# Where an expert's token list is made in a mixture-of-experts layer, and how many semaphores its gathers count on

## The chip, the cores and the metric

The kernel runs on one NeuronCore of one Trainium2 chip. The metric is device time in microseconds (us) for one launch, the median of several runs. One further launch was recorded by the hardware profiler; all rows shown here come from that one.

The engines are called as the profile calls them: PE is the matrix engine (PEld its weight loads), DVE the vector engine, ACT the scalar engine, POOL the GpSimd engine, SP the sync engine, which here only issues DMAs. DMAs that POOL issues run in one queue, those of SP in another.

## The reference

```python
x = x + tanh(g_xattn[0]) * xattn(layernorm(x), ctx_512, ...)      # (32, 112, 256), 16 heads, 375 keys
x = x + tanh(g_ffn[0])   * ffn(layernorm(x), Wg, W1, b1, W2, b2)

def ffn(x, Wg, W1, b1, W2, b2):          # 3584 tokens, 8 experts, k = 896 tokens of each
    S = sigmoid(xt @ Wg).T
    G, I = top_k(S, k)
    ex = xt[I]
    hid = gelu(einsum('ekh,ehf->ekf', ex, W1) + b1[:, None, :])          # 256 -> 1024
    out = (einsum('ekf,efh->ekh', hid, W2) + b2[:, None, :]) * G[..., None]   # 1024 -> 256
    return zeros_like(xt).at[I.reshape(-1)].add(out.reshape(-1, h))
```

Every expert takes its own 896 best tokens, so a token may be taken by several experts or by none.

## The kernel before

The program has four stages one after the other: constants and queries, attention, routing (scores, then a search for each expert's threshold, to about 694 us of the span), and `experts`, to the end. The change is in `experts` alone.

**Tiles of an expert.** Its 896 tokens are 7 groups of 128 rows (`NG`), in two chunks: groups 0 to 3 and groups 4 to 6 (`CHUNK`). Each float32 operand is held as a high and a low part, and each product is three matmuls. The first product (L1266) has 16 rounds of six matmuls: `k = 8 * c + f`, 8 blocks of 128 hidden columns for each chunk. ACT takes each round through Gelu twice (L1156, L1157), DVE subtracts to get the low part (L1203, tile `hl`). The second product (L1278) has 24 matmuls for each of the 7 groups; DVE adds the bias (L1219), ACT multiplies by the gate (L1162), and POOL adds the 128 rows into the output in HBM with an indirect DMA, the scatter (L1133).

**What an expert needs.** Its token list: `list_start` (six DVE instructions, L751 to L761) writes one-hot tiles, `list_rows` (L768, four times) writes masks, `list_products` (L779) is 32 small PE matmuls in four groups of eight, and `list_end` (five DVE instructions, L791 to L796) makes the row numbers `T.idx` and the gates `T.gate`. POOL then copies both (L1120, L1121), and issues seven indirect DMAs, the gathers (L1125), one for each group of 128 rows, from HBM to `ex`. PE transposes `ex` (L1295), ACT and DVE split it into `exh` and `exl` (L1168, L1225). Weights: SP loads W1 and W2 (1 MB each, L815 and L817) into one pair of buffers as soon as the last low part of the weights that lay there is made; ACT makes the high part (L804) and DVE the low part (`weights_low`, L811) in the second product of the expert before.

**The order.** Each engine runs a function `step` for s = -1 to 7, where `live(0)` is expert s, `live(1)` work for expert s + 1, `live(2)` for expert s + 2. Steps 1 to 4 are a hardware loop, the others are written out. Before the change, expert s + 2's list is made in step s: `list_start` after round 1 of the first product, masks after rounds 4, 7, 10 and 13, the 32 matmuls between groups 1 and 2 of the second product, `list_end` after `result(2)`. Expert 0's list is made in routing, expert 1's in step -1, in one piece, while expert 0's rows are gathered. The gathers of expert s + 1 are issued at the start of step s on POOL, ahead of the scatters of expert s.

On PE the second product of a step is: groups 0 and 1, list matmuls, groups 2 and 3, a wait for all seven gathers (`gathered`), transposes of chunk 0, group 4, transposes of chunk 1, groups 5 and 6. On DVE it is `result(g)` and `weights_low` part g for g = 0 to 3, then `tokens_low(0)`, `result(4)`, `tokens_low(1)`, `result(5)`, `result(6)`. All queues are in order.

Of the kernel before, what the change touches and what calls it, by code (L numbers as in the profile page):

```python
# [18 lines left out]
NG = CAP // 128  # L19
# [744 lines left out]
def list_rows(dve, T, at, j):  # L764

    n = B // 4
    wait(dve, T.l_used, at(4, j - 3))
    dve.tensor_tensor(T.L[j][:], T.iota_l[:].unsqueeze(1).to_broadcast([LQ, n, 128]),  # L768
                      T.place_e[:, 1, j * n:(j + 1) * n].unsqueeze(2).to_broadcast([LQ, n, 128]), ALU.is_equal)\
       .then_inc(T.l_ready, 1)  # L770


def list_products(pe, T, at, pR, j):
    pe.wait_ge(T.l_ready, at(4, j + 1))
    if j == 0:
        pe.wait_ge(T.listing, at(LISTING, 6))
    for b in range(B // 4):
        k = j * (B // 4) + b
        last = pe.matmul(pR[:, 0:5 * NG], T.L[j][:, b, :], T.A[:, k].rearrange("p c g -> p (c g)"),  # L779
                         start=(k == 0), stop=(k == B - 1))  # L780
    last.then_inc(T.l_used, 1)
# [258 lines left out]
def experts(nc, T, xn, W1, b1, W2, b2, out):  # L1040

    CHUNK = [(0, 4), (4, NG)]
    with ExitStack() as ctx:
        sem = Sems(nc, ctx, "e")

# [15 lines left out]
        p1, p2, pT, pR = banks("p1", 3), banks("p2"), banks("pT"), banks("pR", 1)[0]  # L1061
        b1_loaded, b1_t, b1_c, b1_e = sem("b1_loaded"), sem("b1_t"), sem("b1_c"), sem("b1_e")
        b2_loaded = [sem("b2_loaded0"), sem("b2_loaded1")]
        gathered, added = sem("gathered"), sem("added")
        xt_ready, xh_done, xl_done = sem("xt_ready"), sem("xh_done"), sem("xl_done")
        h_ready, hh_done, hl_done = sem("h_ready"), sem("hh_done"), sem("hl_done")
        y_ready, y_read, y_done, passed = sem("y_ready"), sem("y_read"), sem("y_done"), sem("passed")
# [15 lines left out]
        def count(i, r, off, per, add):  # L1083
            return i * (2 * per) + ((r + off) * per + add)

        def of(i, r, off):

            return lambda per, add: count(i, r, off, per, add)
# [22 lines left out]
        @block.gpsimd  # L1111
        def _(pool):
            def step(i, r, live):
                if live(1):
                    p = (r + 1) % 2

                    wait_alone(pool, y_done, count(i, r, -1, NG, NG), passed)
                    wait_alone(pool, added, count(i, r, -1, 16 * NG, 16 * NG), passed)
                    wait_alone(pool, T.listing, count(i, r, 1, LISTING, LISTING), passed)
                    pool.tensor_copy(idx[p][:], T.idx[:]).then_inc(T.idx_ready, 1)  # L1120
                    pool.tensor_copy(gate[p][:], T.gate[:]).then_inc(T.idx_ready, 1)  # L1121
                    wait_alone(pool, T.idx_ready, count(i, r, 1, 2, 2), passed)
                    wait_alone(pool, xt_ready, count(i, r, 0, 4, 4), passed)
                    for g in range(NG):
                        pool.indirect_dma_start(out=ex[:, g, :], out_offset=None, in_=xn,  # L1125
                                                in_offset=bass.IndirectOffsetOnAxis(ap=idx[p][:, g:g + 1], axis=0))\
                            .then_inc(gathered, 16)
                if live(0):

                    wait_alone(pool, added, count(i, r, -1, 16 * NG, 16 * NG), passed)  # L1130
                    for g in range(NG):
                        wait_alone(pool, y_done, count(i, r, 0, NG, g + 1), passed)
                        pool.indirect_dma_start(out=out, out_offset=bass.IndirectOffsetOnAxis(ap=idx[r % 2][:, g:g + 1], axis=0),  # L1133
                                                in_=y[g][:], in_offset=None, compute_op=ALU.add).then_inc(added, 16)

            run(pool, step)
            pool.wait_ge(added, NE * NG * 16)
# [51 lines left out]
        @block.vector  # L1189
        def _(dve):  # L1190
            def step(i, r, live):
                new = of(i, r, 2)

                def at(per):
                    return count(i, r, 2, per, 0)

                if live(0):
                    for c, (g0, g1) in enumerate(CHUNK):
                        n = (g1 - g0) * 128
                        for f in range(8):  # L1200
                            k, cols = 8 * c + f, slice(g0 * 128, g1 * 128)
                            dve.wait_ge(hh_done, count(i, r, 0, 16, k + 1))
                            dve.tensor_tensor(hl[:, f, cols], hid[k % 4][:, 0:n], hh[:, f, cols].bitcast(F32),  # L1203
                                              ALU.subtract).then_inc(hl_done, 1)
                            if live(2) and k == 1:
                                list_start(dve, T, new, at)
                            if live(2) and k in (4, 7, 10, 13):
                                list_rows(dve, T, new, (k - 4) // 3)
                    dve.wait_ge(b2_loaded[r % 2], fills(i, r, 0, 16, 16))
                elif live(2):  # L1210
                    list_start(dve, T, new, at)
                    for g in range(4):
                        list_rows(dve, T, new, g)
                    list_end(dve, T, new, pR)

                def result(g):
                    dve.wait_ge(y_ready, count(i, r, 0, NG, g + 1))
                    wait(dve, added, count(i, r, -1, 16 * NG, 16 * NG))
                    dve.tensor_tensor(y[g][:], p2[g % 2][:, 0:D], b2s[r % 2][:], ALU.add).then_inc(y_read, 1)  # L1219

                def tokens_low(c):
                    g0, g1 = CHUNK[c]
                    for kk in range(2):
                        dve.wait_ge(xh_done, count(i, r, 1, 4, 2 * c + kk + 1))
                        dve.tensor_tensor(exl[:, kk, g0 * 128:g1 * 128], pT[kk][:, 0:(g1 - g0) * 128],  # L1225
                                          exh[:, kk, g0 * 128:g1 * 128].bitcast(F32), ALU.subtract).then_inc(xl_done, 1)

                if live(0):
                    for g in range(4):
                        result(g)  # L1230
                        if live(1):
                            weights_low(dve, T, (r + 1) % 2, of(i, r, 1), g)
                        if live(2) and g == 2:
                            list_end(dve, T, new, pR)
                if live(1):
                    tokens_low(0)
                if live(0):
                    result(4)
                if live(1):
                    tokens_low(1)  # L1240
                if live(0):
                    result(5)
                    result(6)

            run(dve, step)

        @block.tensor
        def _(pe):
# [4 lines left out]
            def step(i, r, live):  # L1253
                if live(0):
                    wh, wl = T.w1h[r % 2], T.w1l[r % 2]
                    pe.wait_ge(T.w_low, count(i, r, 0, 4, 4))
                    for c, (g0, g1) in enumerate(CHUNK):
                        n, cols = (g1 - g0) * 128, slice(g0 * 128, g1 * 128)
                        pe.wait_ge(xl_done, count(i, r, 0, 4, 2 * c + 2))
                        for f in range(8):  # L1260
                            if 8 * c + f >= 3:
                                pe.wait_ge(hh_done, count(i, r, 0, 16, 8 * c + f - 2))
                            fs, j = slice(f * 128, (f + 1) * 128), 0
                            for k in range(2):
                                for w, v in ((wh, exh), (wh, exl), (wl, exh)):
                                    last = pe.matmul(p1[(8 * c + f) % 3][:, 0:n], w[:, k, fs], v[:, k, cols], start=(j == 0), stop=(j == 5))  # L1266
                                    j += 1
                            last.then_inc(h_ready, 1)

                def second(g0, g1):  # L1270
                    for g in range(g0, g1):
# [7 lines left out]
                                j += 1  # L1279
                        last.then_inc(y_ready, 1)  # L1280

                new = of(i, r, 2)
                if live(0):
                    second(0, 2)
                if live(2):
                    for j in range(4):
                        list_products(pe, T, new, pR, j)
                if live(0):
                    second(2, 4)

                def transposes(c):
                    for kk in range(2):
# [4 lines left out]
                        last.then_inc(xt_ready, 1)  # L1297

                if live(1):
                    pe.wait_ge(gathered, count(i, r, 1, 16 * NG, 16 * NG))  # L1300
                    transposes(0)
                if live(0):
                    second(4, 5)
                if live(1):
                    transposes(1)
                if live(0):
                    second(5, NG)
# [46 lines left out]
```

## Time and profile before

| | us |
|---|---|
| median of 3 runs (1063.42 to 1067.46) | 1063.61 |
| the profiled execution | 1062.17 |
| its span, first to last instruction | 1060.4 |
| PE busy over the span | 885.8 (84%) |
| DVE / ACT / POOL busy | 698.5 / 616.3 / 227.5 |
| granted PE clock, mean of the span | 0.928 of full |

Times in the rows are us from the start of the span. In a timeline the first number is the start and the second the length. For a row with "x2" or more it is the length of them together. A bracket at the end gives the idle time before the instruction and what ended it. The granted clock is 1.00 at 2.4 GHz and 0.50 at 1.2 GHz.

### The profile page before, as it was taken

Reading aid. Unit: us, or ns where it says so; the run is one execution under the profiler, and the core shown is the slowest. Engines: PE = TensorE matmul, PEld = TensorE weight load, DVE = VectorE, ACT = ScalarE, POOL = GpSimd, SP = SyncE. Lnnn points to the kernel's source line nnn. Section 1 sums busy time; section 2 is a strip of 40 time slices with the busy share of each in tenths; the row PEclk is TensorE's granted clock in tenths of the full one; section 3 lists DMA queues with packets and bytes.
Section 4 is the critical chain, followed back from the end, with each engine's and each line's share of the span. In section 5 each row is a group of like instructions: output and inputs, shape, how many; then the busy total and the mean of one; then the engine's idle time right before and its main releaser. Section 6 shows DMA issues by size and latency. Waiting matters only on the chain. (4 is left out here: it accounts for less than half of the span.)

```text
span 1060.4 us, 23352 instructions
## 1 busy us (share of the span) xinstructions
PE 885.8 (84%) x8843; PEld 700.0 (66%) x8843; DVE 698.5 (66%) x1884; ACT 616.3 (58%) x1305; POOL 227.5 (21%) x192
## 2 busy tenths in 40 slices
PE   0763789999999999999999850039999999999995
PEld 0331357767676776777676640029999999999995
DVE  6681267787778777877878648857566576574540
ACT  1432477777777777777776531009568476485671
POOL 1343000000000000000000004042556466565313
PEclk9986699999999999999999975559999999999998
DMA  2211674565566456546644012031533524525203
GB/s 69 70 35 35 154 161 116 143 156 124 118 156 143 122 131 157 129 121 147 151 114 101 24 34 77 0 127 34 125 83 95 128 46 123 128 49 137 40 11 35
DMA packets 96209, 104.63 MB, mean 99 GB/s; under 512 B 11744, under 2 KB 92272, under 8 KB 96112
## 3 DMA queue, kind: packets, MB, share of 16 engines
q1 hardware_dynamic: 84128, 88.50, 33.5%
q0 software_dynamic: 10752, 14.69, 8.1%
q8 instruction: 65, 1.06, 0.4%
q10 hardware_dynamic: 1232, 0.12, 0.1%
q14 instruction: 32, 0.26, 0.1%
HBM read 39.60 MB, written 14.68 MB: 51 GB/s over the span
## 5 line engine op out<-in xcount | busy, mean ns | idle before, releaser
L405 DVE TENSOR_REDUCE a_nm<-a_pS 112x1 f32<-112x375 f32 x512 | 264.7, 543 | 122.8 <-PE a_pS L500 119.8
L350 ACT ACTIVATE a_P<-a_pT 128x448 f32<-128x448 f32 x384 | 209.2, 546 | 136.0 <-PE a_pT L494 135.3
L500 PE MATMUL a_pS<-kst,a_qst 96*112 96x375 bf16 x512 | 151.9, 336 | 3.6 <-DVE a_nm L405 3.1
L494 PE MATMUL a_pT<-a_qst,kst 98*128 98x112 bf16 x1536 | 139.3, 213 | 1.6 <-DMA a_qst<-a_mT 1.5
L494 PEld LDWEIGHTS a_pT<-a_qst,kst 98*128 98x128 bf16 x1536 | 107.4, 99 | 42.7 <-issue 8.6
L1278 PE MATMUL e_p<-w2h,e_hh 128*128 128x256 f32 x448 | 128.3, 286 | 0.0
L1278 PE MATMUL e_p<-w2h,e_hl 128*128 128x256 f32 x448 | 126.2, 282 | 0.0
L1278 PE MATMUL e_p<-w2l,e_hh 128*128 128x256 f32 x448 | 126.2, 282 | 0.0
L358 ACT ACTIVATE kp<-a_pK,bk 128x375 bf16<-128x375 f32 x192 | 109.5, 570 | 19.1 <-PE a_pK L524 12.1
L1133 POOL DMA_INDIRECT out_dram<-e_y,e_idx x56 | 88.3, 1577 | 134.0 <-ACT e_y L1162 130.3
L879 POOL MEMSET r_factors<- 128x1 f32 x15 | 0.6, 98 | 540.2 <-POOLq L236 539.9
L1203 DVE TENSOR_TENSOR e_hl<-e_hid,e_hh 128x384 fp32r<-128x384 f32 (+1 forms) x128 | 77.7, 623 | 52.9 <-ACT e_hh L1157 52.2
L511 PE MATMUL a_pO<-a_P,V 128*32 128x112 f32 (+1 forms) x3072 | 100.9, 264 | 0.3 <-ACT a_P L350 0.3
L1266 PE MATMUL e_p<-e_exh,w1h 128*128 128x512 f32 (+1 forms) x256 | 94.8, 370 | 0.0
L1266 PE MATMUL e_p<-e_exl,w1h 128*128 128x512 f32 (+1 forms) x256 | 94.5, 369 | 0.0
L1266 PE MATMUL e_p<-e_exh,w1l 128*128 128x512 f32 (+1 forms) x256 | 94.5, 369 | 0.0
L1125 POOL DMA_INDIRECT e_ex<-xn_scratch,e_idx x56 | 82.8, 1478 | 27.3 <-issue 15.6
L1156 ACT ACTIVATE e_hid<-e_p,e_b1e 128x384 f32<-128x384 f32 (+1 forms) x128 | 81.5, 637 | 9.7 <-PE e_p L1266 1.5
L1278 PEld LDWEIGHTS e_p<-w2l,e_hh 128*128 128x128 f32 x448 | 84.7, 189 | 0.0
L1278 PEld LDWEIGHTS e_p<-w2h,e_hl 128*128 128x128 f32 x448 | 84.5, 189 | 0.0
L1278 PEld LDWEIGHTS e_p<-w2h,e_hh 128*128 128x128 f32 x448 | 84.1, 188 | 0.0
L511 PEld LDWEIGHTS a_pO<-a_P,V 128*32 128x32 f32 (+1 forms) x3072 | 69.8, 110 | 21.6 <-issue 20.3
(193 smaller groups left out, 1506.3 us busy)
## 6 DMA issues: line engine op xcount, KB each, us to landing
kst<-kp SPq DMA_DIRECT2D x192, 192.0 KB, 3.6
w<-in_L_ffn_W_dram SPq DMA_DIRECT2D x16, 1024.0 KB, 7.5
a_qst<-qp SPq DMA_DIRECT2D x96, 112.0 KB, 3.8
a_craw<-in_ctx_dram SPq DMA_DIRECT2D x32, 128.0 KB
q_xin<-in_x_dram SPq DMA_DIRECT2D x8, 448.0 KB, 3.8
a_xb<-in_x_dram SPq DMA_DIRECT2D x32, 112.0 KB, 3.2
out_dram<-a_x SPq DMA_DIRECT2D x32, 112.0 KB, 2.5
xn_scratch<-a_x SPq DMA_DIRECT2D x32, 112.0 KB, 2.6
```

What stands on the lines that cost most here:

```text
L350: act.activation(P[quad % 2][:, c, :], pT[u % 2][:, 0:4 * LQ], ACT.Exp).then_inc(exp_done, 1)
L358: act.activation(kp[b % 2][:, part, t, 0:LK], pK[:, 0:LK], ACT.Identity, bias=T.bk[:, t:t + 1])\
L405: dve.tensor_reduce(nm[:, h:h + 1], pS[h % 2][0:LQ, 0:LK], AXX, ALU.max, negate=True).then_inc(s_used, 1)
L494: last = pe.matmul(pT[u % 2][:, j * LQ:(j + 1) * LQ], kst[b % 4][:, h, c * 128:(c + 1) * 128], q_of(b, slice(None), h), start=True, stop=True)
L500: pe.matmul(pS[h % 2][0:LQ, 0:LK], q_of(b, slice(0, ROWS), h), kst[b % 4][0:ROWS, h, 0:LK], start=True, stop=True).then_inc(s_ready, 1)
L511: last = pe.matmul(pO[VW * j:VW * (j + 1), quad * LQ:(quad + 1) * LQ], V[b % 2][0:n, c, 4 * quad + j, :], P[quad % 2][0:n, c, j * LQ:(j + ...
L1125: pool.indirect_dma_start(out=ex[:, g, :], out_offset=None, in_=xn, in_offset=bass.IndirectOffsetOnAxis(ap=idx[p][:, g:g + 1], axis=0))\
L1133: pool.indirect_dma_start(out=out, out_offset=bass.IndirectOffsetOnAxis(ap=idx[r % 2][:, g:g + 1], axis=0), in_=y[g][:], in_offset=None, c ...
L1156: act.activation(hid[k % 4][:, 0:n], p1[k % 3][:, 0:n], ACT.Gelu, bias=b1e[:, f:f + 1])
L1203: dve.tensor_tensor(hl[:, f, cols], hid[k % 4][:, 0:n], hh[:, f, cols].bitcast(F32), ALU.subtract).then_inc(hl_done, 1)
L1266: last = pe.matmul(p1[(8 * c + f) % 3][:, 0:n], w[:, k, fs], v[:, k, cols], start=(j == 0), stop=(j == 5))
L1278: last = pe.matmul(p2[g % 2][:, 0:D], v[:, f, rows], w[:, f, :], start=(j == 0), stop=(j == 23))
```

## The change

The list of expert s + 1 is made in step s instead of step s - 1, all of it before the second product. `list_start` comes after round 0, the masks after rounds 3, 6, 9 and 11, and PE's four groups of eight list matmuls after rounds 6, 9, 12 and 14 of the first product. `list_end` comes on DVE after the last `hl` of the first product, ahead of `result(0)`. Step -1 makes no list. The gathers count on two semaphores: groups 0 to 3 on `gathered[0]`, groups 4 to 6 on `gathered[1]`; PE waits for the second only ahead of the transposes of chunk 1. POOL's order is the same: copies, seven gathers, seven scatters.

```diff
+    ROWS_AT, LISTED_AT = [3, 6, 9, 11], [6, 9, 12, 14]
-        gathered, added = sem("gathered"), sem("added")
+        gathered, added = [sem("gathered0"), sem("gathered1")], sem("added")
@@ gpsimd
-                            .then_inc(gathered, 16)
+                            .then_inc(gathered[int(g >= CHUNK[1][0])], 16)
@@ vector
-                new = of(i, r, 2)
+                new = of(i, r, 1)
                 def at(per):
-                    return count(i, r, 2, per, 0)
+                    return count(i, r, 1, per, 0)
...
-                            if live(2) and k == 1:
+                            if live(1) and k == 0:
                                 list_start(dve, T, new, at)
-                            if live(2) and k in (4, 7, 10, 13):
-                                list_rows(dve, T, new, (k - 4) // 3)
+                            if live(1) and k in ROWS_AT:
+                                list_rows(dve, T, new, ROWS_AT.index(k))
+                    if live(1):
+                        list_end(dve, T, new, pR)
                     dve.wait_ge(b2_loaded[r % 2], fills(i, r, 0, 16, 16))
-                elif live(2):
-                    list_start(dve, T, new, at)
-                    for g in range(4):
-                        list_rows(dve, T, new, g)
-                    list_end(dve, T, new, pR)
...
-                        if live(2) and g == 2:
-                            list_end(dve, T, new, pR)
@@ tensor
                             last.then_inc(h_ready, 1)
+                            if live(1) and 8 * c + f in LISTED_AT:
+                                list_products(pe, T, of(i, r, 1), pR, LISTED_AT.index(8 * c + f))
...
-                new = of(i, r, 2)
                 if live(0):
-                    second(0, 2)
-                if live(2):
-                    for j in range(4):
-                        list_products(pe, T, new, pR, j)
-                if live(0):
-                    second(2, 4)
+                    second(0, 4)
...
                 if live(1):
-                    pe.wait_ge(gathered, count(i, r, 1, 16 * NG, 16 * NG))
+                    pe.wait_ge(gathered[0], count(i, r, 1, 16 * 4, 16 * 4))
                     transposes(0)
                 if live(0):
                     second(4, 5)
                 if live(1):
+                    pe.wait_ge(gathered[1], count(i, r, 1, 16 * 3, 16 * 3))
                     transposes(1)
```

## Rows read from the trace of the kernel before

**Rows 1.** The chain that ended last, in order: start, us, what.

```profile
705.33 3.59 DMA e_ex<-xn_scratch,e_idx
...
711.55 1.69 PE e_pT L1295 x6
713.24 21.34 PE e_p L1266 x96
...
757.15 19.58 PE e_p L1266 x96
776.73 5.75 PE e_p L1278 x48
782.48 0.82 PE e_pR L779 x32
783.30 5.84 PE e_p L1278 x48
789.14 0.87 PE e_pT L1295 x8
790.01 2.87 PE e_p L1278 x24
...
987.49 11.52 PE e_p L1278 x96
```

**Rows 2.** Timeline of POOL, the copies and gathers ahead of expert 0.

```profile
694.94 0.24 POOL L1120 COPY e_idx<-idx 128x7 int32<-128x7 int32 x1 [41.64 <-POOLq L826]
...
695.81 1.33 POOL L1125 DMA_INDIRECT e_ex<-xn_scratch,e_idx  x1 [0.50 <-POOL e_gate L1121]
...
701.57 0.95 POOL L1125 DMA_INDIRECT e_ex<-xn_scratch,e_idx  x1 [0.30 <-issue]
```

**Rows 3.** Timeline of DVE, expert 1's masks in step -1.

```profile
696.96 4.62 DVE L768 TENSOR_TENSOR L<-iota_l,place_e 112x1024 bf16<-112x1024 f32 x4
```

**Rows 4.** Timeline of DVE in step 1, whose first product ends at 776.73.

```profile
777.38 1.03 DVE L1203 TENSOR_TENSOR e_hl<-e_hid,e_hh 128x384 fp32r<-128x384 f32 x2
...
780.08 1.22 DVE L811 TENSOR_TENSOR w1l<-w,w1h 128x1024 fp32r<-128x1024 f32 x1
...
787.77 0.19 DVE L791 COPY rt<-e_pR 128x35 f32<-128x35 f32 x1
...
788.70 0.40 DVE L796 TENSOR_SCALAR gate<-gate,gf 128x7 f32<-128x7 f32 x1
```

**Rows 5.** Timeline of POOL in step 3, a copy and a gather beside DVE work.

```profile
848.19 1.45 POOL L1121 COPY e_gate<-gate 128x7 f32<-128x7 f32 x1
850.66 2.50 POOL L1125 DMA_INDIRECT e_ex<-xn_scratch,e_idx  x1 [1.03 <-issue]
```

**Rows 6.** Timeline of DVE in the same stretch of step 3.

```profile
848.30 1.29 DVE L1203 TENSOR_TENSOR e_hl<-e_hid,e_hh 128x512 fp32r<-128x512 f32 x2
...
851.57 0.69 DVE L1203 TENSOR_TENSOR e_hl<-e_hid,e_hh 128x512 fp32r<-128x512 f32 x1
```

**Rows 7.** Timeline of SP's queue, weight loads issued in steps -1 and 0.

```profile
696.21 0.38 SPq L815 DMA_DIRECT2D w<-in_L_ffn_W_dram  x1
...
748.86 0.39 SPq L815 DMA_DIRECT2D w<-in_L_ffn_W_dram  x1
```

**Rows 8.** DMA issue to landing, us, issued at 695.8, 714.0, 745.4 and 749.2.

```profile
e_ex<-xn_scratch,e_idx POOLq DMA_INDIRECT x1, 7.7
...
e_ex<-xn_scratch,e_idx POOLq DMA_INDIRECT x1, 2.7
...
out_dram<-e_y,e_idx POOLq DMA_INDIRECT x1, 3.8
...
out_dram<-e_y,e_idx POOLq DMA_INDIRECT x1, 8.3
```

**Rows 9.** Stretches: length, busy of PE, PEld, DVE, ACT, POOL, clock, DMA share, GB/s.

```profile
1048.00:1051.00 3.00, 0.88 (x8) 0.68 (x6) 0.42 (x1) 0.51 (x1) 1.68 (x2) 1.00 0.37 44
1051.00:1052.00 1.00, 0.00 (x0) 0.00 (x0) 0.00 (x0) 0.00 (x0) 0.71 (x1) 0.77 0.00 0
```

## The prediction

> **What bounds the kernel now.** I read the chain of waits first, since it says which stage the change can move. From 713.24 to the last matmul it is PE alone [rows 1]: in the whole stage PE never waits, and a step lasts 42.15 us, 19.58 of it the first product. So whatever the change puts on PE, or makes PE wait for, is paid in full, and what it speeds on other engines in the steps gives nothing. The reader is to see one more thing in the chain: ahead of the first expert it runs over the gathers and their last landing, at 708.92 (705.33 + 3.59), then 4.3 us of transposes and splits before the first product [rows 1]. There the change can win. The timelines of POOL and DVE then show what lies beside these pieces, and the DMA issues with their landings what a gather costs at different times.
>
> I write E for the end of a step's first product (776.73 in step 1, [rows 1]) and give later times as E + x.
>
> **Ahead of the first expert: a gain of 4.0.** The seven gathers are issued from 695.81; the first took 1.33 us, the fourth 0.95 and each has 0.30 idle before it [rows 2]. The slow ones lie beside expert 1's masks on DVE [rows 3], which go. At 1.25 each the fourth starts at 699.56 instead of 701.57 and the seventh at 703.32 instead of 705.33. The weights are in flight then (issued at 696.21, [rows 7]), so landings don't move as far as issues; I take the seventh at 707 (bounds: 2.7 after its issue, 706.0, by the gather without a load beside it [rows 8], and 708.9, unmoved). With the second semaphore the transposes of chunk 0 and their splits run before that: they took from 708.96 to 711.51 for the half that the next transposes wait for. Only the last 1.69 us of transposes stays behind the landing [rows 1]. With the fourth landed at 705 the first product starts at about 707.5 + 1.7 = 709.2, not 713.24: 4.0 won. Ends: 2.6 (708.9 + 1.7) and 5.5.
>
> **PE's list work: 2.4 lost.** Groups 0 to 3 of the second product take 5.75 + 0.82 + 5.84 with the list between them and 11.52 without [rows 1]: 0.89 for a list, of which 0.07 is the seam. Six lists lay in steps before, seven do now: 0.9. Four seams in place of one: 3 x 0.07 x 7 = 1.5. Whether the masks are ready costs nothing if they are: the fourth, after round 11, would be done about 18.6 us into the step and PE asks for it after round 14, at about 19.3; the others have 0.5 to 1.0 us too. If that cover is gone, each late mask costs its lateness, up to 0.5 in four places of seven steps; I take the sum as 0.9 to 6.
>
> **The new wait: 34 lost.** This is the heart. List and gathers of expert s + 1 were a step ahead; now they start when the first product has ended, and PE asks for the first four gathers 11.5 us later, at E + 11.5, and for the last three 0.87 + 2.87 us after that, at E + 15.3 [rows 1]. Followed step by step:
> - The last `hl` ends at E + 1.7. `list_end` takes 1.33 (787.77 to 789.10), so the list is ready at E + 3.0 in the loop; a written-out step has 0.23 in place of 0.40 for its last instruction and is ready at E + 2.75 [rows 4].
> - POOL's copy starts 0.3 later. A POOL copy beside DVE's subtraction is held until that ends: it took 1.45 and ended at 849.64, the subtractions at 849.59 [rows 5, 6]. In the new place DVE starts the first `weights_low` at E + 3.35 and ends it at E + 4.57 [rows 4]. In the loop the gate's copy meets it; 1.0 us of waits follows [rows 5]: first gather at E + 5.7. In a written-out step the copy is through, and the first gather itself is held to E + 4.5.
> - A gather that starts beside a subtraction is held the same way: 2.50 instead of 0.95, up to the end of the one that ends at 852.26 [rows 5, 6]. The next `weights_low` parts lie at about E + 6.1, 9.1 and 11.95, 1.22 each. With 1.25 a gather and these holds, the fourth works from E + 8.5 (loop: 10.1), the seventh from E + 13.05 (loop: 14.3).
> - The fourth lands 2.7 to 2.8 later [rows 8]: at E + 11.3, in time; in the loop at E + 13.0, 1.5 late.
> - The seventh meets the weights. SP issues their load when the fourth `weights_low` ends: at 748.86 in step 0, E + 14.3 [rows 7], and now 0.8 to 0.9 sooner, at E + 13.4, since no list stands in the second product. A gather issued 0.4 before such a load landed after 7.7 instead of 2.7. A scatter issued 0.4 behind it landed after 8.3 instead of 3.8 [rows 7, 8]. I take 7.0 to 7.3 after issue: E + 20.2, and E + 21.3 in the loop. PE asks at E + 15.3 and at E + 16.8 there: it waits 4.8 and 4.5.
>
> The sum: steps 0 and 5, 4.8 each; steps 1 to 4, 6.0 each; step 6 has no load left, 0.6: 34.2. Bounds: with every landing at 2.7 and no copy held it is 0 to 0.6 a step, under 4 in all; with 8.3 it is 45.
>
> By the row the POOL queue stands nearly still while the weights pour in. The Trainium skill, "DMA: Bandwidth & Descriptors", section "Queues, rings and completion order", says otherwise: each DMA engine goes round its queues and changes after a packet, so a gather would wait for a packet or so of the weights and land within a microsecond of its usual time. That would make the sum the one of the first rival.
>
> **PE's clock: 11 lost.** The granted clock was 1.00 (2.4 GHz) until PE had done its last matmul at 1048.9, and fell in the slice from 1051, mean 0.77, with PE idle from the one to the other [rows 9]. A wait of 4.5 to 5 us in six steps is longer than that idle time and should bring it to 0.50 each time. The nearest price is the first product of expert 0, begun at the low level: 21.34 instead of 19.58 [rows 1], so 1.8 a time, 10.8 for six. Ends: nothing, and 20 if the low stretch covers twice that work.
>
> What else moves costs nothing that I can see. POOL's seven scatters stand behind the gathers and end at about E + 29 instead of E + 26; they are asked for when the next step's list is copied, at E + 45. The second product's DVE work loses `list_end` from its middle. The first product's DVE work is the same, shifted by a round.
>
> **Sum.** 1062.2 (profiled) - 4.0 + 2.4 + 34.2 + 10.8 = 1105.6. The median of the runs is 1.4 above the profiled one: 1107.0.
>
> **Rivals.**
> - *The gathers slip past the weights* (the other side). They land 2.7 to 3.6 after issue, because the seventh is ahead of the load by a few tenths, or since it gets its turn. For it: the scatter at 745.4, 3.5 us ahead of a load, had its usual 3.8 [rows 8]. Against it: the seventh starts only 0.35 ahead, nearer to the gather that took 7.7. Then the waits are 0.3 to 0.6 a step, the clock stays: 1063.6 - 4.0 + 2.4 + 4 = 1066. The point from which it decides is the seventh gather working by about E + 12, in place of 13.05. 0.15.
> - *The same, and everything in time:* no wait, PE's seams free: 1063.6 - 5.5 + 0.9 = 1059, and 1058 with the clock up sooner in the first product. 0.05.
> - *Only the loop's late start costs.* No meeting with the weights, but the held copy and 1.8 a step in four steps: 9 + 2.4 - 4.0: 1071. 0.12.
> - *Forecast:* the weights catch the seventh gather in at least steps 0 to 5. Without the clock's loss 1096, with stalls of 6 and the larger clock price 1124. 0.68.
>
> **Chances and range.** A measurement of this kernel can tell about 0.5%, 5.3 us. Faster by more than that: 0.05, the second rival. Within it: 0.15, the first. Slower: 0.80, the other two. The range from 1066 to 1122 takes in the third and half of the first, and leaves out its upper end, where every unknown is dear; the forecast's own range is 1086 to 1122.
>
> **What would show it.** In the changed kernel's chain: the first product of expert 0 starts near 709; gathers stand in the chain of every step; PE's transposes of chunk 1 wait 4 to 5 us in steps 0 to 5 and under 1 in step 6; the landing of the gathers issued last in a step is near 7 in the first six. Stretches of 0.50 clock follow these waits. The forecast is wrong if DVE doesn't hold POOL (all gathers issued by E + 12.5), or if those landings stay near 3.

## The result, and the profile after

| | before | after |
|---|---|---|
| median of 6 runs each | 1063.69 us | 1096.03 us |
| ratio | 1 | 1.0297, 95% interval 1.0271 to 1.0323 |
| profiled execution / its span | 1062.17 / 1060.4 | 1094.03 / 1092.3 |
| PE busy (share of the span) | 885.8 (84%) | 897.3 (82%) |

The change costs 32.3 us, 3.0%. The forecast was 1107, 11 us too much; its range held. The ratios here and below leave out a run that lies over 1.5% above the fastest of its kernel; that happened once, in `a_w2_first`.

PE was busy for 11.5 us more, and the rest of the time is in waits. Those of PE from 700 us on are these (who waited, for whom: us in total, times, longest):

```profile
PE e_pT L1287 <- DMA e_ex<-xn_scratch,e_idx: 29.3, 9, 8.9
PE e_pT L1287 <- DVE e_exl L1223: 0.7, 1, 0.7
```

8.9 of the 29.3 lie ahead of expert 0, where the kernel before had 6.9. The other 20.4 are new. The chain shows where (start, us, what), from the end of step 1's first product, which I call E as in the prediction (780.08):

```profile
780.08 8.65 PE e_p L1276 x72
...
791.44 0.95 POOL e_ex L1126
792.39 0.30 issue
792.69 6.10 DMA e_ex<-xn_scratch,e_idx
798.79 0.05 issue
798.84 1.02 PE e_pT L1287 x6
799.86 7.10 PE e_p L1276 x48
806.96 9.82 PE e_p L1262 x42
816.78 0.21 PE e_pR L779 x8
817.00 3.58 PE e_p L1262 x18
820.58 0.21 PE e_pR L779 x8
820.79 3.23 PE e_p L1262 x18
824.02 0.21 PE e_pR L779 x8
824.23 2.17 PE e_p L1262 x12
826.40 0.21 PE e_pR L779 x8
826.62 1.16 PE e_p L1262 x6
```

The reader is to see three things against [rows 1]. A gather, the seventh, now stands in the middle of the second product, with 6.10 us from issue to landing. Behind it 48 matmuls take 7.10 us, not 5.75. And the list's four groups of eight stand in the first product, which lasts 20.82 (806.96 to 827.77) instead of 19.58.

POOL's timeline of that step, with SP's queue behind it:

```profile
783.00 0.19 POOL L1121 COPY e_idx<-idx 128x7 int32<-128x7 int32 x1 [20.91 <-DVE gate L796]
783.13 0.18 POOL L1122 COPY e_gate<-gate 128x7 f32<-128x7 f32 x1
784.31 1.24 POOL L1126 DMA_INDIRECT e_ex<-xn_scratch,e_idx  x1 [1.00 <-POOL e_gate L1122]
...
788.56 0.96 POOL L1126 DMA_INDIRECT e_ex<-xn_scratch,e_idx  x1 [0.30 <-issue]
...
792.69 1.31 POOL L1126 DMA_INDIRECT e_ex<-xn_scratch,e_idx  x1 [0.30 <-issue]
```
```profile
793.42 0.37 SPq L815 DMA_DIRECT2D w<-in_L_ffn_W_dram  x1
793.99 0.37 SPq L817 DMA_DIRECT2D w<-in_L_ffn_W_dram  x1
```

The DMA issues with their landings, for the gathers issued at 791.44, 792.69 and 1031.17 (the seventh of step 6, which loads no weights):

```profile
e_ex<-xn_scratch,e_idx POOLq DMA_INDIRECT x1, 2.7
...
e_ex<-xn_scratch,e_idx POOLq DMA_INDIRECT x1, 6.1
...
e_ex<-xn_scratch,e_idx POOLq DMA_INDIRECT x1, 3.2
```

Neighbours 1.25 us apart in one queue land after 2.7 and after 6.1. The weight load is issued 0.73 behind the second of them. In steps 0 to 5 the seventh gather landed after 5.5, 6.1, 5.9, 6.0, 6.5 and 6.0 us.

The clock, in three stretches behind that wait (length, busy of PE, PEld, DVE, ACT, POOL, clock, DMA share, GB/s):

```profile
794.00:799.00 5.00, 1.62 (x14) 1.41 (x13) 0.81 (x2) 0.51 (x1) 4.08 (x4) 1.00 0.87 293
799.40:802.80 3.40, 3.40 (x18) 3.40 (x17) 1.03 (x2) 0.96 (x2) 2.79 (x3) 0.50 1.17 278
802.80:806.90 4.10, 4.10 (x36) 4.10 (x35) 0.42 (x1) 0.51 (x1) 1.63 (x2) 1.00 0.63 83
```

After a stretch with 1.62 us of work in 5, PE had 1.2 GHz for about 3.4 us, with 18 matmuls in 3.4 us, and then 36 in 4.1. In the second product one matmul started 0.21 us after another at the low level, and 0.12 at the high one. There is one such stretch after the wait in each of steps 1 to 5, and none in step 0, whose wait came as 1.2 and 1.45 us in two pieces. The first piece was for the fourth gather, which landed 4.2 us after its issue, with no weight load issued by then; the trace names no reason.

**Where the 29.6 us went.** From the first gather's issue to the last matmul the kernel before took 353.1 us (695.81 to 1048.90), the one after 382.7 (698.04 to 1080.78). The 2.2 by which that first issue came later lie in routing, which the change doesn't touch.

| part | predicted | measured |
|---|---|---|
| ahead of expert 0 | -4.0 | -2.6 |
| list matmuls: 7 x 1.24 less 6 x 0.89 | +2.4 | +3.3 |
| first product of expert 0, clock up sooner (20.7 from its first matmul without the list, not 21.7) | 0 | -1.0 |
| PE's waits for gathers, steps 0 to 6: 2.7, 3.4, 3.3, 3.4, 3.9, 3.4, 0.5 | +34.2 | +20.4 |
| low clock: 5 stretches, about 1.5 each | +10.8 | +7.4 |
| not placed (0.3 a step) | | +2.1 |

### The profile page after: what moved, and what is told of

Its sections match the earlier page's. It is cut to its first block and busy times, and to the rows that moved or that the text cites. A ratio compares the mean times of both kernels' runs of the same rounds, so it can differ in the third digit from the quotient of the medians.

```text
span 1092.3 us, 23365 instructions
## 1 busy us (share of the span) xinstructions
PE 897.3 (82%) x8843; PEld 705.2 (65%) x8843; DVE 698.5 (64%) x1884; ACT 616.9 (56%) x1305; POOL 201.7 (18%) x192
## 5 line engine op out<-in xcount | busy, mean ns | idle before, releaser
L1276 PE MATMUL e_p<-w2h,e_hh 128*128 128x256 f32 x448 | 131.2, 293 | 0.0
L1276 PE MATMUL e_p<-w2h,e_hl 128*128 128x256 f32 x448 | 129.9, 290 | 0.0
L1276 PE MATMUL e_p<-w2l,e_hh 128*128 128x256 f32 x448 | 129.4, 289 | 0.0
L358 ACT ACTIVATE kp<-a_pK,bk 128x375 bf16<-128x375 f32 x192 | 109.5, 570 | 19.1 <-PE a_pK L524 12.1
L1157 ACT ACTIVATE e_hid<-e_p,e_b1e 128x384 f32<-128x384 f32 (+1 forms) x128 | 81.6, 637 | 17.8 <-PE e_p L1262 10.8
L1276 PEld LDWEIGHTS e_p<-w2l,e_hh 128*128 128x128 f32 x448 | 88.6, 198 | 0.0
L1276 PEld LDWEIGHTS e_p<-w2h,e_hh 128*128 128x128 f32 x448 | 88.0, 197 | 0.0
L1276 PEld LDWEIGHTS e_p<-w2h,e_hl 128*128 128x128 f32 x448 | 87.8, 196 | 0.0
L1163 ACT ACTIVATE e_y<-e_y,e_gate 128x256 f32<-128x256 f32 x56 | 28.5, 508 | 99.1 <-DVE e_y L1217 99.1
```

The lines of the kernel that those rows point to most:

```text
L358: act.activation(kp[b % 2][:, part, t, 0:LK], pK[:, 0:LK], ACT.Identity, bias=T.bk[:, t:t + 1])\
L1157: act.activation(hid[k % 4][:, 0:n], p1[k % 3][:, 0:n], ACT.Gelu, bias=b1e[:, f:f + 1])
L1276: last = pe.matmul(p2[g % 2][:, 0:D], v[:, f, rows], w[:, f, :], start=(j == 0), stop=(j == 23))
```

## The experiments

Ratios are to the kernel before, run on the same chip. The runs of one kernel scatter over some 8 us, so the steps are compared by their traces.

**1. The load behind the gathers** (`a_load_late`): one more wait of SP in the kernel after.

```diff
                     wait_alone(sp, T.w_low, count(i, r, 0, 4, 4), passed)
+                    wait_alone(sp, gathered[1], count(i, r, 0, 16 * 3, 16 * 3), passed)
                     load_weights(...)
```

> The changed kernel, but SP also waits for the last three gathers of expert s before it issues the load of expert s + 1's weights. Theory (the weight load holds up the seventh gather in POOL's queue): the seventh gather lands 2.7 to 3.2 us after its issue instead of 5.5 to 6.5, PE waits under 1 us a step, the granted clock stays at 1.00 in the steps, and the kernel takes 1064 to 1068. Rival (POOL's queue is slow by itself there, with scatters issued right behind the gather): landings stay near 6, time stays near 1096. Second rival (the later load is missed later, at the next expert's casts of the weights): the stall moves to the end of the next first product, 1075 or more.

Measured: 1072.09 us, ratio 1.0070 (1.0049 to 1.0091). The seventh gather of step 1:

```profile
790.64 3.71 DMA e_ex<-xn_scratch,e_idx
794.39 0.87 PE e_pT L1288 x6
795.27 5.76 PE e_p L1277 x48
```

Landing 3.7 instead of 6.1, 48 matmuls again in 5.76, no low clock in any step, and 24 us gained by moving a transfer of 2 MB to a later time. The edit also holds back the load ahead of expert 0: 2.8 of the gain lie there (11.7 us from the first gather's issue to the first product instead of 14.5), 20.5 behind. That names the load as the cause of most of the loss. The scatters right behind the gathers are still there, so POOL's own queue isn't it. But 1072 is above what I expected: waits of up to 1.1 us were left in the steps, 5.3 us in all. Experiment 5 takes that up.

**2. The list earlier** (`a_list_early`): the load stays, the gathers come sooner.

```diff
-    ROWS_AT, LISTED_AT = [3, 6, 9, 11], [6, 9, 12, 14]
+    ROWS_AT, LISTED_AT = [2, 4, 6, 8], [5, 7, 9, 11]
...
-                    if live(1):
-                        list_end(dve, T, new, pR)
+                            if live(1) and k == 11:
+                                list_end(dve, T, new, pR)
```

> The changed kernel with the list earlier in the same first product: masks after rounds 2, 4, 6 and 8, list matmuls after rounds 5, 7, 9 and 11, list_end after round 11. The load stays where it is. Theory: the list is ready some 5 us earlier, the seventh gather is issued near E + 8.5, ahead of the load at E + 13.4, and lands in about 3; no wait on PE, 1063 to 1067. Rival (the list in the first product costs PE much, by seams or late masks): 1070 or more although the gathers are in time.

Measured: 1066.08 us, ratio 1.0018 (0.9989 to 1.0047). The seventh gather is issued at E + 6.9 to 9.1, and the load at E + 13.2 or later finds all landed. PE waits for no gather in the steps:

```profile
778.05 11.52 PE e_p L1276 x96
789.57 0.87 PE e_pT L1287 x8
790.45 2.87 PE e_p L1276 x24
793.32 0.66 PE e_pT L1287 x6
793.97 5.75 PE e_p L1276 x48
799.73 8.42 PE e_p L1262 x36
```

So it isn't the move into the predecessor's first product that costs the 3%, but its last few microseconds: the point named in the prediction's first rival. What remains is 42.47 a step against 42.15 in steps 1 to 5, the list's seams.

**3. What the second semaphore is worth.** `b_two_sems` is the kernel before with it, `a_one_sem` the kernel after without.

```diff
-                            .then_inc(gathered, 16)
+                            .then_inc(gathered[int(g >= CHUNK[1][0])], 16)
...
-                    pe.wait_ge(gathered, count(i, r, 1, 16 * NG, 16 * NG))
+                    pe.wait_ge(gathered[0], count(i, r, 1, 16 * 4, 16 * 4))
                     transposes(0)
...
+                    pe.wait_ge(gathered[1], count(i, r, 1, 16 * 3, 16 * 3))
                     transposes(1)
```

> The kernel before with the two semaphores alone. Theory: ahead of expert 0, PE's first product starts 2.6 us earlier against the first gather's issue, with the last landing unmoved, and nothing changes in the steps: 1061 (ratio 0.9975). Rival (the gain there came from the masks taken away from DVE): under 0.5 us won, 1063.5.

> The changed kernel with one semaphore for all seven gathers, as before. Theory: PE waits at E + 11.5 for the landing at about E + 18.7, so group 4 and the transposes of chunk 0 (3.7 us) no longer lie under it: 3.7 x 7 + 2.6 = 28 us more than the changed kernel, about 1124, and some more if the low clock lasts longer. Rival (the second semaphore matters only ahead of expert 0): 1099.

`b_two_sems`: 1063.07 us, 0.9977 (0.9956 to 0.9999). Ahead of expert 0 its trace shows 1.0 us won, not the 2.6 expected. `a_one_sem`: 1128.13 us, 1.0598 (1.0554 to 1.0642), so in the new order the second semaphore is worth 32 us, 4 more than expected. The chain of `a_one_sem` in step 2 shows why it is more:

```profile
850.76 6.74 DMA e_ex<-xn_scratch,e_idx
857.54 1.97 PE e_pT L1287 x8
859.51 3.57 PE e_p L1276 x24
863.09 0.66 PE e_pT L1287 x6
```

PE stands 7.9 us for the seventh landing, where group 4 and the first transposes lay under it before, and comes back at the low clock: eight transposes in 1.97 instead of 0.87.

Ahead of expert 0 the four kernels give, from the first gather's issue to the first matmul of the first product: before 17.1, the semaphore alone 16.1, the masks away alone (`a_one_sem`) 17.3, both (after) 14.5. Only both together give 2.6. One profile each, and landings there differ by 1 us between runs, so the split between the two isn't settled.

**4. What holds the gather up.** Three kernels change what meets it. `a_w2_first` issues W2 (rows of 1 KB) ahead of W1 (rows of 4 KB). `a_w1_late` issues W2 at the usual time and W1 after the gathers. `a_256k` issues only a quarter of W2 then (`between` is the wait for `gathered[1]` of `a_load_late`):

```diff
+    w2 = W2.rearrange("e f d -> (e f) d")[rows2].rearrange("(k p) d -> p k d", k=8)
+    sp.dma_start(T.w2[:, 0:2], w2[:, 0:2]).then_inc(T.w_loaded, 16)
+    between()
+    sp.dma_start(T.w2[:, 2:8], w2[:, 2:8]).then_inc(T.w_loaded, 16)
     sp.dma_start(T.w1[:], ...).then_inc(T.w_loaded, 16)
```

> The changed kernel with the two parts of each weight load swapped: W2 (rows of 1 KB) is issued first, W1 (rows of 4 KB) second. In the changed kernel W1 went first and the seventh gather landed 5.5 to 6.5 us after issue. Theory A (the size of the load's packets sets how long POOL's queue is held up): with 1 KB packets in front the seventh gather lands in 3 to 4, PE waits about 1 us a step, 1074 or so. Theory B (whatever is in line must be moved first): landings stay near 6, time near 1096.

> The changed kernel with W2 issued where the whole load was, and W1 only after the last three gathers have landed. Only 1 MB meets the seventh gather. Theory A (packet size): landing 3 to 4, as with W2 first. Theory B (bytes in line): landing 4.5 to 5, half of the added 3.3 us, and PE waits about 2 us a step, 1080.

> The changed kernel with only 256 KB of W2 issued where the whole load was; the rest follows once the last three gathers have landed. Until here, gathers caught by a load of 1 or 2 MB had their first row moved 3.8 to 5.4 us after issue in place of 1.7, with 220 to 940 KB of the load moved before it. Theory (the load must be moved first, up to some amount): 256 KB take about 1 us, so caught gathers land at most 4.5 after issue. Rival (a fixed hold of 2 to 4 us follows each issue of SP, whatever its size): landings of 5.4 to 6.9 as before in the steps in which the load is issued under 1.5 us after the gather.

Times: `a_w2_first` 1085.65 us, ratio of the other three runs 1.0165 (1.0111 to 1.0219), with runs from 1077.9 to 1097.7, of which the slowest is the one traced, so that other runs may have gone better than its trace; `a_w1_late` 1087.17, 1.0222 (1.0174 to 1.0270); `a_256k` 1074.08, 1.0084 (1.0053 to 1.0115). From the DMA packets in the traces, for the seventh gather of a step (us; load issue and packets counted from the gather's issue):

| kernel, step | gather's time on POOL | load issued | load's first packet | gather's first packet / its last one ends | load moved before the gather's first |
|---|---|---|---|---|---|
| after, 1 | 1.31 | 0.73 | 1.75 | 4.4 / 5.6 | 724 KB |
| after, 5 | 1.31 | 0.57 | 1.59 | 4.8 / 5.6 | 942 KB |
| `a_w2_first`, 1 | 1.98 | 1.40 | 2.44 | 4.4 / 5.3 | 397 KB |
| `a_w2_first`, 3 | 0.96 | 1.73 | 2.63 | 1.68 / 2.43 | 0 |
| `a_w1_late`, 2 | 1.98 | 1.42 | 2.47 | 4.0 / 5.3 | 303 KB |
| `a_w1_late`, 4 | 0.95 | 1.34 | 2.49 | 1.67 / 2.49 | 0 |
| `a_one_sem`, 2 | 1.99 | 1.43 | 2.49 | 4.9 / 6.2 | 647 KB |
| `a_one_sem`, 3 | 0.96 | 1.75 | 2.52 | 1.67 / 2.47 | 0 |
| `a_256k`, 1 | 1.31 | 0.73 | 1.75 | 2.8 / 3.5 | 203 KB |

I call a gather caught when packets of the load come ahead of its own. A caught gather has its first packet at 3.8 to 5.5 in all kernels with 1 MB or 2 MB in the load, and lands after 5.4 to 6.9. The theory of packet size (A) falls, since with 1 KB rows in front the landing isn't 3 to 4. They help a little: against `a_one_sem`, whose gathers stood on POOL as long, the first packet in `a_w2_first` came 0.2 to 0.7 sooner in steps 0, 2, 4 and 5.

Theory B foresaw landings near 6 there, but not that half the bytes would help no more: with 1 MB they are 5.4, 5.8 and 6.8, not 4.5 to 5. The table's last column says why. At most 942 KB were moved ahead of any caught gather, so the second megabyte never stood in its way.

The theory of the third run holds: with 256 KB the first packet comes at 2.6 to 3.1, when 202 to 214 of the 262 KB are moved, and the landing is 3.6 to 4.1. So the hold grows with the load up to somewhere between 256 KB and 1 MB, and hardly beyond. What sets that limit the runs don't show.

The second reading of the table: it is all or nothing, and DVE has a part in it. In steps 0 to 5 of four kernels (after, `a_w2_first`, `a_w1_late`, `a_one_sem`) 18 of 24 gathers were caught. All 18 had been held on POOL by a subtraction (1.3 to 2.0 us instead of 0.95). The six that weren't held all escaped, with the load issued 1.3 to 2.4 behind them. Without a load, a gather held for the full 2.0 us has its first packet at 2.6 to 2.7 (`a_load_late`), one that isn't held at 1.7. With the load's packets from 2.5 on, the one comes too late and the other in time. In the kernel after all six were held and the load's packets came at 1.6 to 1.8. One gather doesn't fit an order by first packets: in step 4 of `a_w2_first` the load's first packet came at 2.9, and the gather, held for 1.97, still waited until 5.1.

That the held gathers stood 1.3 us in the kernel after and 1.8 to 2.0 in the other three has its own cause: `result(3)`, and with it the subtraction behind it and the load, came later there. In each step of the three it started at E + 12.1 to 13.0 instead of 11.55, and the load was issued at E + 13.8 to 15.1 instead of 13.2 to 13.4. In step 1 of `a_w1_late` `result(3)` started 1.4 us behind the end of PE's last matmul of group 3. The traces name no reason for that.

**5. What DVE costs the gathers** (`a_low_later`): `a_load_late`, with the four `weights_low` moved out of the gathers' time (`low(k)` is `weights_low` part k).

```diff
                     for g in range(4):
                         result(g)
-                        if live(1):
-                            weights_low(dve, T, (r + 1) % 2, of(i, r, 1), g)
...
                     tokens_low(0)
+                low(0)
                     result(4)
+                low(1)
                     tokens_low(1)
+                low(2)
                     result(5)
+                low(3)
                     result(6)
```

> The changed kernel with the load behind the gathers, and with DVE's four weights_low moved from between result(0) and tokens_low(0) to behind tokens_low(0). It asks what DVE's subtractions cost POOL's gathers. Theory (a gather that meets one is held until it ends): with none in the way the seventh gather is issued at E + 12.0 instead of 12.8, takes 0.95 instead of 2.0, lands by E + 15, PE waits for nothing in the steps, and the kernel takes 1065 to 1067 instead of 1072. Rival (the gathers' pace is POOL's own): issue at E + 12.8 and 1072 again. Second rival (weights_low now comes too late for the next first product): PE waits there, 1072 or more.

Measured: 1062.16 us, ratio 0.9978 (0.9952 to 1.0005): 10 us less than `a_load_late`, a little more than expected. In `a_load_late` the seventh gather and the subtraction beside it were:

```profile
790.64 2.00 POOL L1127 DMA_INDIRECT e_ex<-xn_scratch,e_idx  x1 [0.30 <-issue]
```
```profile
790.60 1.22 DVE L811 TENSOR_TENSOR w2l<-w,w2h 128x1024 fp32r<-128x1024 f32 x1
```

The subtraction began 0.04 earlier, and the gather took 2.00. In `a_low_later`, step 1, the last three gathers:

```profile
783.27 0.95 POOL L1127 DMA_INDIRECT e_ex<-xn_scratch,e_idx  x1 [0.30 <-issue]
784.53 0.95 POOL L1127 DMA_INDIRECT e_ex<-xn_scratch,e_idx  x1 [0.30 <-issue]
785.78 0.95 POOL L1127 DMA_INDIRECT e_ex<-xn_scratch,e_idx  x1 [0.30 <-issue]
```

The seventh is issued at E + 11.9 and lands 2.8 later, PE waits for no gather in steps 0 to 5, and the steps last 42.50 us. With load and subtractions out of the way the whole is as fast as the kernel before, but not because the new order is free. From the first gather's issue to the first product it takes 11.7 us against 17.1, and from there to the last matmul 339.3 against 336.0. The 3.3 are the list's matmuls, paid by a gain ahead of expert 0 that experiment 7 has without the new order.

**6. The list's seams** (`a_early_one_seam`): `a_list_early` with its 32 list matmuls together.

```diff
-                            if live(1) and 8 * c + f in LISTED_AT:
-                                list_products(pe, T, of(i, r, 1), pR, LISTED_AT.index(8 * c + f))
+                            if live(1) and 8 * c + f == LISTED_AT[3]:
+                                for q in range(4):
+                                    list_products(pe, T, of(i, r, 1), pR, q)
```

> The changed kernel with the list earlier (masks after rounds 2, 4, 6 and 8, list_end after round 11), and its 32 list matmuls all together after round 11 instead of in four groups. Theory (each group costs its matmuls, 0.21, and a seam of 0.1): the first product of a listing step lasts 20.5 us instead of 20.8, and the kernel 1064. Rival (the 1.24 us come from the number of list matmuls or from waits on masks): 20.8 again, or a wait on PE.

The first product lasts 20.50 instead of 20.80, as expected: a seam is 0.1 us, not the 0.07 of the prediction. The time shows nothing of it: 1066.45 us, 1.0003 (0.9973 to 1.0034), where 1064 was expected. Several of its steps lasted 0.6 to 2.0 us longer than 42.2, where PE's second product had small gaps that nothing in the trace ends.

**7. The version that beats both** (`b_two_late`): the kernel before with the two semaphores and with the load behind the gathers, as in experiments 3 and 1. It touches only what lies ahead of expert 0.

> The kernel before with the two semaphores, and the load of expert s + 1's weights issued only after expert s's last three gathers have landed. This changes only what lies ahead of expert 0, since in the steps the gathers landed long before the load. Theory: there the gathers land in about 3 us instead of 3.6 to 7.7, the first product starts some 3 to 4 us sooner than with the two semaphores alone, 1059 (ratio 0.996). Rival (the weights of expert 1 come too late): no gain.

Measured: 1059.56 us, ratio 0.9959 (0.9935 to 0.9984). The chain ahead of expert 0, against [rows 1] and [rows 2]:

```profile
694.08 1.33 POOL e_ex L1126
...
703.60 2.71 DMA e_ex<-xn_scratch,e_idx
706.31 0.04 issue
706.35 1.54 PE e_pT L1296 x6
707.90 20.88 PE e_p L1267 x96
```

From the first gather's issue to the first matmul of the first product it takes 13.5 us where the kernel before took 17.1 and `b_two_sems` 16.1. That is 2.6 us less than with the semaphores alone, a little under the 3 to 4 expected, and the last landing took 2.71 as without a load. The steps last 42.15 us as before.

## Why the prediction was right, and where its sizes were not

- **PE's path decides, and the new waits stand on it:** right. PE had no wait in the steps before, 20.4 us of them after, and experiments 2 and 5 take those of steps 0 to 5 away in two ways, experiment 1 all but 5.3 us.
- **The weights catch the seventh gather in steps 0 to 5, not in step 6:** right, in each step. It landed after 5.5 to 6.5, behind 140 to 230 rows of 4 KB of the load, 9 to 14 for each of the 16 DMA engines. The prediction set against this the Trainium skill, "DMA: Bandwidth & Descriptors", "Queues, rings and completion order": a DMA engine goes round its queues packet by packet. From that it worked out a landing in 3 to 4, and this estimate was wrong. The rule itself isn't refuted: the same section gives a packet as typically 9 to 17 descriptors and at most 64, and if a descriptor is one row, that is by estimate 0.6 to 1.1 MB of 4 KB rows on 16 engines, where 0.57 to 0.94 MB were moved. With 1 KB rows 13 to 47 for each engine were moved, mostly more than the typical packet and always under its limit. No run here shows where a packet of that kind ends.
- **The size of the hold was taken too large.** The step at fault is the choice of 7.0 to 7.3 from the gather at 695.8 and the scatter at 749.2 [rows 8]; the gathers took 5.5 to 6.5. Both models have something besides the load: the one has two more transfers of SP in flight with it, the other is a read and a write. That this made them slower is my guess; no run separates it. It made 4.8 and 4.5 a step where 2.7 to 3.9 were paid, some 7 us in all. The upper bound beside it was off as well: with landings of 8.3 the prediction's own terms give about 41, not 45.
- **The gate's copy isn't held in the loop.** The prediction took the list's last instruction at 0.40 in the loop [rows 4]; in the new place it took 0.23, the copy ran at 783.13, and `weights_low` began at 783.43. It was 0.1 us early instead of late. With it fell the 1.5 us at the first wait in four steps, 6 us. In step 0, where the fourth gather was to land 0.2 ahead of PE, it came 1.2 late without a load beside it. This cost nothing by itself, since the seventh landed later still. An outcome that hangs on a tenth should have been carried as two cases.
- **POOL held by DVE's subtractions:** right in mechanism, shown in experiment 5, and in size: the seventh gather's work was foreseen from E + 13.05 in the written-out steps, and it ran from 792.69 (E + 12.6) with 0.36 of holding.
- **The load is issued at E + 13.4:** right, E + 13.2 to 13.4.
- **The clock:** right in kind. Five times and 1.5 us each, not six times and 1.8. Step 0's wait, split in two by the late fourth gather, left it at 2.4 GHz, which is luck as far as the prediction goes.
- **Ahead of expert 0:** 2.6 instead of 4.0, the low end named. The issues came closer together as worked out (the seventh 7.75 behind the first, not 9.52), but its landing stayed 13.1 behind the first issue in both kernels. With the load in flight, issuing sooner gains no landing; that failed step was to let it move from 708.9 to 707.
- **The list's matmuls:** 3.3 instead of 2.4, since a seam is 0.1.
- **What was missed:** that the hold by DVE and the catch by the load work together. The prediction counted the first as 0.4 us of delay; its greater effect in experiment 4 is that the gather's packets come behind the load's. In the kernel after the load's first packet came at 1.6 to 1.8, about when that of a gather that isn't held does (1.7), so there the runs don't show that a gather not held would have escaped.

## What to carry to other kernels

Before moving work later in a step, list what each queue issues around the new time, not only what the moved work waits for: the 2 MB load that nobody waited for cost more than all the moved instructions. Where a small transfer on the critical path and a large one that has time share the DMA engines, let the large one wait for the small one; here one wait turned +3.0% into +0.7%, and 0.3 of these 2.3 points were won ahead of expert 0. And where two events lie within some tenths of a microsecond in the plan, price both orders.

## What the runs showed of the hardware that I had not expected

- A gather of 128 rows in POOL's queue, caught by a load of 1 or 2 MB from SP's queue, had its first packet 3.8 to 5.5 us after issue; without a load 1.7, or 2.6 to 2.7 if held on POOL. Rows of 1 KB in the load's front, in place of 4 KB, brought it forward by 0.2 to 0.7 only. With a load of 256 KB it came at 2.6 to 3.1.
- A gather is caught whole or not at all. With the load's first packet 2.47 and 2.49 us behind the gather's issue, a gather held on POOL for 1 us by a DVE subtraction was caught, and one not held escaped (`a_w1_late`, steps 2 and 4).
- Waits of 3.3 to 3.9 us on PE brought one stretch of about 3.4 us at 1.2 GHz behind each; the wait of 1.2 and 1.45 us with 4.0 us of work between brought none, and one of 7.9 us brought 6.8 us (`a_one_sem`, step 2).
